# The diffusion's reciprocal seed in a PSUM bank instead of an SBUF tile

## The reference, cut to what matters

```
x = x + diffusion(group_norm(x))            # layer 0, element by element with neighbours
x = x + deformable_conv(group_norm(x))      # layer 1, 9 taps, bilinear samples at computed places
```

```
g, g1  = relu(bn(dwconv3x3(h))) , twice     # two gates
gy, gx = sobel(h)
Dx, Dy = 1/(gy*gy/4 + 1) , 1/(gx*gx/4 + 1)
Bx, By = 0.2*Dx , 0.2*Dy
D      = 1/(1 + 2*Bx + 2*By)
h      = 5 steps of D*(c0*h0 - 2*E*h + cm_x*left + cp_x*right + cm_y*below + cp_y*above) + D*0.4*f
return relu(bn(h))
```

## Time and profile before

| what | value |
| --- | --- |
| median of 3 runs (lowest, highest) | 796.09 us (794.35, 797.31) |
| span of the profiled execution, first to last instruction | 791.9 us |
| POOL busy, instructions | 550.6 us (70%), 589 |
| PE busy, instructions | 675.1 us (85%), 4714 |
| DVE busy, instructions | 533.5 us (67%), 901 |
| ACT busy, instructions | 242.8 us (31%), 471 |
| POOL busy on line 606 alone | 540.1 us, 568 instructions |
| exponential, line 1176, mean | 616 ns |
| mean granted TensorE clock | 0.909 of full speed |

### The profile page before, as it was taken

One profiled execution on the slowest core, in us unless ns is written; L12 is line 12 of the kernel. 1 busy time (PEld: TensorE's weight loads), 2 busy tenths in 40 slices (PEclk: granted clock), 3 DMA queues, 4 the chain that ended last, 5 costly groups with the idle time before them and its releaser, 6 DMA issues.

```text
span 791.9 us, 14534 instructions
## 1 busy us (share of the span) xinstructions
PE 675.1 (85%) x4714; PEld 596.5 (75%) x4714; DVE 533.5 (67%) x901; ACT 242.8 (31%) x471; POOL 550.6 (70%) x589
## 2 busy tenths in 40 slices
PE   8998888899899989998798989988798987564665
PEld 6877668798788888888777877878788977454555
DVE  4785578777977897788667796678667885222122
ACT  4514421543154214522254214412254213000000
POOL 2203777777777777777777777777777777777774
PEclk9999889999999999999899998999899998555557
DMA  5103333533453435343454335343354335433332
GB/s 168 57 4 98 107 110 108 161 110 110 115 161 112 123 109 165 108 128 108 115 157 129 108 114 159 114 122 107 112 162 114 109 112 161 116 109 113 107 109 73
DMA packets 55139, 92.75 MB, mean 117 GB/s; under 512 B 13384, under 2 KB 35480, under 8 KB 55064
## 3 DMA queue, kind: packets, MB, share of 16 engines
q0 software_dynamic: 27264, 74.49, 32.4%
q1 hardware_dynamic: 27064, 16.93, 7.7%
q10 hardware_dynamic: 736, 0.41, 0.2%
HBM read 79.37 MB, written 12.40 MB: 116 GB/s over the span
## 4 chain that ended last, share of the span: by engine, by line
POOL 42%; PE 24%; issue 17%; DVE 14%; ACT 2%; DMA 1%; POOLq 0%; DVEq 0%; SPq 0%; ACTq 0%
POOL pixels L606 42%; PE banks L1247 16%; PE banks L1250 8%; DVE weighted L984 3%; DVE prod L892 1%; DVE prod L874 1%; DVE banks L835 1%; DVE prod L880 1%; DVE prod L855 1%; DMA pixels<-table,index 1%; DVE prod L854 1%; DVE row_squares L622 1%; ACT coef_T L1136 0%; DVE xn L666 0%; DVE xc L650 0%
## 5 line engine op out<-in xcount | busy, mean ns | idle before, releaser
L606 POOL DMA_INDIRECT pixels<-table,index x568 | 540.1, 951 | 204.2 <-issue 172.2
L1250 PE MATMUL banks<-const,weighted 128*128 128x128 f32 x1280 | 193.6, 307 | 54.9 <-DVE weighted L984 44.6
L984 DVE TENSOR_TENSOR weighted<-pixels,banks 128x2304 f32<-128x2304 f32 (+1 forms) x65 | 161.1, 2479 | 116.3 <-DMA pixels<-table,index 112.6
L1250 PEld LDWEIGHTS banks<-const,weighted 128*128 128x128 f32 x1280 | 168.5, 163 | 65.8 <-DVE weighted L984 48.8
L1148 ACT ACTIVATE sampled_T<-banks 128x512 f32<-128x512 f32 (+1 forms) x128 | 55.8, 436 | 327.5 <-PE banks L1250 327.5
L1250 PE MATMUL banks<-const,prod 128*128 128x128 f32 x816 | 110.3, 278 | 14.1 <-DVE prod L854 7.3
L1250 PEld LDWEIGHTS banks<-const,prod 128*128 128x128 f32 x816 | 90.9, 143 | 22.8 <-DVE banks L836 8.6
L1247 PE MATMUL banks<-conv_w,xT 128*128 128x64 f32 (+2 forms) x576 | 97.7, 325 | 0.7 <-ACT banks L1125 0.7
L1247 PEld LDWEIGHTS banks<-conv_w,xT 128*128 128x128 f32 x576 | 91.4, 191 | 7.0 <-ACT banks L1125 1.6
L1247 PE MATMUL banks<-filt,sampled_T 128*128 128x64 f32 x640 | 88.0, 288 | 7.2 <-ACT sampled_T L1148 7.2
L1247 PEld LDWEIGHTS banks<-filt,sampled_T 128*128 128x128 f32 x640 | 82.5, 204 | 13.6 <-ACT sampled_T L1148 11.5
(11 more groups left out here) (159 smaller groups left out, 675.9 us busy)
## 6 DMA issues: line engine op xcount, KB each, us to landing
far_pixels<-table SPq DMA_DIRECT2D x1024, 1.0 KB
pixels<-table,index POOLq DMA_INDIRECT x568, 2.7
table<-xn SPq DMA_DIRECT2D x46, 128.0 KB
table<-xn SPq DMA_DIRECT2D x16, 144.0 KB
x<-x_in SPq DMA_DIRECT2D x30, 64.0 KB, 2.4
out_dram<-x SPq DMA_DIRECT2D x60, 32.0 KB
table<-corner_w SPq DMA_DIRECT2D x16, 70.0 KB
const<-const_in SPq DMA_DIRECT2D x2, 384.0 KB, 4.5
```

The lines of the kernel that those rows point to most:

```text
L606: pool.indirect_dma_start(out=pixels[:, col % NB, k, :], out_offset=None, in_=table[0:(u + 1) * TY * TX, :], in_offset=bass.IndirectOffset ...
L984: return dve.tensor_tensor(weighted[:, col % 2, :, a:b, :].rearrange("p q k c -> p k q c"), entries.rearrange("p k (q c) -> p k q c", c=C) ...
L1250: return pe.matmul(dst, data, moved, start=start, stop=stop, is_transpose=True, skip_group_check=True)
```

## The change

`seed_arr` is no longer the second plane of `work` but bank 2 of PSUM. The logarithm is written there by ACT, the exponential read and written there, and DVE's lines 731 and 732 read `t` or its successor from SBUF and the seed from PSUM. Since bank 2 was last used for `row` of the image before, `log` gets a second wait: for DVE to have emptied it. Nothing else changes; the number and the order of the instructions on each engine are the same.

```
-        t_arr, seed_arr, d_gates = work[:, 0, :], work[:, 1, :], work
+        t_arr, d_gates = work[:, 0, :], work
...
-        dp, delta = b_sq, b_sq
+        dp, delta, seed_arr = b_sq, b_sq, banks[:, 2, :]
...
                 elif name == "log":
                     act.wait_ge(s_t, n + 1)
+                    if n:
+                        act.wait_ge(*emptied(n - 1, "row"))
                     seq(act.activation(seed_arr, t_arr, ACT.Ln, bias=log_const))
                     prepare()
```

## The result

The changed kernel takes 792.83 us (median of 22 runs, 789.25 to 795.21), the kernel before 795.46 us in the same comparison (22 runs, 793.22 to 797.32). The ratio is 0.9973, with a 95% interval from 0.9962 to 0.9984: 2.1 us less, and between 1.3 and 3.0 (the two medians alone lie 2.6 apart). The prediction said 793.7 us and a gain of 2.4, and took anything under 4 us for too little to be told from no change; with 22 runs of each kernel, 2.1 us can be told.

The account below looks back on a forecast made before the run. POOL's unbroken row of 568 gathers was taken to bound the kernel, between start and tail. Removing 2.4 us of stalls, all else nothing, gave span 791.9 - 2.4 = 789.5 and median 796.09 - 2.4 = 793.7 us; 8-in-10 range 791.8 to 796.4.

Parts of the forecast that it names:

- POOL's row of gathers: POOL, line 606: 568 gathers run without a wait from 69.7 to 782.6 us, between start and tail.
- The seven losses: Gathers held up beside lines 731 and 732 in images 1 to 7: 2.4 us together, coming off one for one.
- the bound of 0.5 us: Five long gathers beside corner-weight instructions: could go (-0.5 us) or rise by about as much (+0.4).
- Which instructions hold: DVE instructions with two SBUF inputs hold a gather starting in their first 0.56 us; one SBUF input almost wholly excluded.
- The room for POOL to be early: Slots and indices for POOL up to 2.4 us sooner: tightest slot 7.7 us ahead, image 1's indices 4.5 us.
- waits longer than 0.31 us: On POOL: new waits of this length, not there before, would make the working as a whole wrong.
- ScalarE and the start: Logarithm and exponential: some 0.1 us less per image, covered by a wait in image 0, so nothing at the start.
- The tail: After the last gather, 9.3 us: PE's clock rise varies between executions; 1 us either way in the forecast's own range.
- Rival 2: Slower: columns 62 and 63 at 1.2 GHz cost 4.4 us, median 798.1 us; chance 0.08.
- Small sizes: Durations: exponential from 616 to between 560 and 588 ns, lines 731 and 732 at 688 to 692 ns.
- The 65 ns more for PSUM on DVE: Lines 731 and 732: fixed cost about 60 ns on SBUF, 125 on PSUM; 1.0 us for 16 instructions, not borne out.
- the 4.2 us between span and median: Whole kernel: the runs' median lies 4.2 us above the span before, taking span 789.5 to median 793.7 us.

Follow-up runs that it names:

- long_psum: Changed kernel plus one 2560-element maximum on DVE in each of images 3 to 7, second input in PSUM; 792.66 us, ratio 0.9955 to the kernel before.
- long_two_sbuf: Changed kernel plus one 2560-element maximum of two SBUF tiles on DVE in each of images 3 to 7; 802.22 us, ratio 1.0091 to the kernel before.
- act_part: Kernel before with only ScalarE's half: logarithm to PSUM, seed back in SBUF, lines 731 and 732 unchanged; 795.77 us, ratio 1.0007.
- tail_warm_before: Kernel before plus 8, 10 and 10 matmuls of ones behind the filters of columns 59, 60 and 61; 793.84 us, ratio 0.9991.
- changed_again: The changed kernel repeated, nothing else altered; 793.13 us, ratio 0.9973 to the kernel before.
- half_newton: Kernel before with line 731's result in PSUM bank 2 and the seed still in SBUF; 794.27 us, ratio 0.9978.
- corner_strong: Changed kernel, corner tiles in PSUM, 14 matmuls of ones behind each filter of columns 57 to 61, 4 behind 62; 791.48 us, ratio 0.9952.
- strong_again: Repeat of changed kernel with corner tiles in PSUM and extra matmuls behind columns 57 to 62; 791.44 us, ratio 0.9960 to the kernel before.
- corner_only: Changed kernel with corner-weight tiles bottom and top in PSUM bank 7; 793.39 us, ratio 0.9975 to the kernel before.
- long_copy: Changed kernel plus one 2560-element SBUF-to-SBUF copy on DVE in each of images 3 to 7; 796.98 us, ratio 1.0032 to the kernel before.

## Why the prediction was right

*POOL's row of gathers sets the time.* Confirmed from both sides: 14 us more of DVE work cost nothing that can be told (long_psum), and 9.9 us of lost gather time came out at 9.6 us more time by the medians and 10.8 by the ratios (long_two_sbuf to long_psum).

*The seven losses are lines 731 and 732, 2.4 us, and come off one for one.* Confirmed. They are gone in the profile, half of the step leaves those of line 731 alone, and the interval of the measured gain, 2.1 us [1.3, 3.0], holds 2.4. The 2.4 is the sum of one execution, and where gathers meet the pair differs: act_part and tail_warm_before lost 2.0. The last gather was to start at 779.3 and starts at 779.4. That close a hit is luck in part: 2.4 us for the pair, 0.5 for the corner weights and 0.4 for the earlier start, less the wait of 1.0, happen to make 2.3. The absolute time has a like share of it: 796.09 was the median of three runs, 0.6 above that of 22. POOL's time on the line fell by 2.9 us, not 2.4, because the corner-weight losses were missing in this execution too; this is the bound of 0.5 us that I had put on them, and the repeat had 0.4 us of such.

*Which instructions hold* was right for this kernel and too narrow as a rule: the copy of one input holds as well. No term of the sum hung on it. The prediction's evidence for it, that a single SBUF input doesn't hold a gather up, came from instructions with one input in PSUM (line 733 and the `mult`s), and those hold nobody up in any profile.

*The room for POOL to be early* is the step that failed in part. The prediction named the right condition, image 1's indices, and put its room at 4.5 us from one execution, with PE at 2.4 GHz until 95 us. It left out the 0.76 us that lie between the indices and the gather, which makes that room some 4 us, and it took it for fixed. In the changed kernel's profile the indices came 4.5 us later and POOL waited 1.0 us, the "waits longer than 0.31 us" that the prediction named as what would upset it. The change isn't enough to cause it: the same kernel waited nowhere in changed_again, and act_part, with the losses still in, waited too (0.7 us). The row of gathers is unbroken only while PE keeps its pace until image 1.

*ScalarE and the start.* Confirmed: from image 0's logarithm to the first gather it is 49.00 us before and after. Line 731 follows the logarithm's start by 2.73 us instead of 2.79, and the wait behind it takes that up.

*The tail* was read rightly as a source of spread larger than the gain, but 1 us either way was too narrow for a single execution: the tail after the last gather lies between 9.2 and 13.6 us in the fourteen profiles. Rival 2's price was paid in part in the profiled run, 2.7 us more tail against 4.4 for the whole of it. In the medians the sign stayed. The prediction's reason, that the kernel before has such tails too, fits act_part (13.6) and half_newton (13.5), but the only profile of the kernel before itself has the short one (9.3), so for it this stays argued.

*Small sizes.* The exponential took 558 ns where I expected 560 to 588; lines 731 and 732 took 685 and 686 ns where I expected 688 to 692. Both are hidden. The 65 ns more for PSUM on DVE, which follow from the Trainium skill's page "Perfetto Trace Analysis", section "Optimizing Scalar/DVE Operations", did not show: the two are 4 and 6 ns shorter. And the 4.2 us between span and median were not all time outside the span: in each of the 22 runs of the changed kernel time and span lie 2.1 to 2.3 us apart. If that holds for the kernel before, its profiled execution was some 2 us faster than its median of 796.09; by what part of it is not shown.

## What to carry to other kernels

When GpSimd does nothing but issue gathers, and does it without a pause, look for the few that are longer than the median and lay VectorE's timeline beside them. An instruction with two SBUF inputs that starts just before a long one is the first suspect, and here moving one of its inputs to PSUM removed the loss at no price. What such an instruction costs doesn't follow from its busy time alone: it costs only where a gather would start inside it, and then what is left of it at that point, but for its last 0.13 us. And where a gain is smaller than the spread of single executions, one profile of each kernel says where the time went, not whether there is less of it.

## What the runs showed of the hardware that I had not expected

- Against a VectorE instruction with two SBUF inputs a gather is open to delay only at its very start: one already under way was never longer, and one that would start inside went on some 0.13 us before the instruction's end (0.56 us after its start for 512 elements and 0.69 us, 2.69 for 2560 and 2.83 us).
- Against a plain float32 copy at the double rate a gather can be held up although it is under way: three that had begun 0.10 to 0.38 us before a copy ended 0.12 us after it. The copy itself can be delayed (1.63 us instead of 1.50, once).
- The start of the first gather moves between executions of one kernel: corner_strong and strong_again are the same, with 69.66 and 67.50 us, and line 731 in image 0 is 2.3 us apart in them already. Over all profiles it lies between 67.4 us (corner_only) and 70.5 (long_copy). This start, image 1's indices and the tail are three places that vary; that they make up the whole spread of some 6 us of one kernel is not shown.
